# Expert layers of a macaron network: the rows of the last two items added to the residual by TensorE products

## Chip, cores and metric

The kernel runs on one core of one Trainium2 chip. The metric is the time of one execution on the device, in microseconds (us); lower is better. Five engines work on their own instruction streams and wait for each other by semaphores: TensorE (PE in the profile, its weight loads PEld), VectorE (DVE), ScalarE (ACT), GpSimd (POOL) and SyncE (SP, which here only issues DMAs).

## What is computed

The input x has 1024 tokens of 256 values, all float32. Six layers follow one another, each adding to the residual x:

```
x = x + 0.5 * L0_ffn(layernorm(x))     # expert layer 0
x = x +       L0_attn(layernorm(x))    # attention, 32 heads of 8
x = x + 0.5 * L0_ffn(layernorm(x))     # expert layer 1, same weights
x = x + 0.5 * L1_ffn(layernorm(x))     # sparse ffn
x = x +       L1_attn(layernorm(x))    # state space layer
x = x + 0.5 * L1_ffn(layernorm(x))     # sparse ffn
```

The change lies in the two expert layers:

```
logits = 30 * tanh(x @ w_gate / 30);  probs = softmax(logits)
mask = one_hot(top_k(probs, 2)).sum;  weights = probs * mask
for e in range(8):
    h = silu(x @ w1[e]) * (x @ w3[e])            # 256 -> 512
    out = out + h @ w2[e] * weights[:, e:e+1]    # 512 -> 256
```

## The kernel before, in words

The residual `xres` stays in SBUF as [128, 8, 256]: 8 tiles of 128 tokens. `moe_layer` (line 175) is called twice, as moe0 and moe1. Only the two chosen experts of each token are computed. The 2048 pairs of token and expert are sorted by expert into items of 128 rows; each expert's last item is padded, so there are at most `ITEMS` = 2048/128 + 8 - 1 = 23 items, and always 23 are computed. The column `token[:, i]` holds the number of the token of each row of item i (numbers from 1024 on are spare rows, for padding), `slot_w[:, i]` half the router's weight of each row.

Five instruction streams make up the layer. SyncE copies the residual to the DRAM tensor `sums` (L262), loads the weights, and at the end waits until all additions have landed (L269) and loads `sums` back into `xres`, two tiles in each of four DMAs (L271). GpSimd gathers the rows of an item from the normalized tokens in DRAM (L283), four items ahead, and adds the 128 result rows of an item to `sums` with one indirect, accumulating DMA (L293). An addition waits for y of its item and for the landing of the addition before it, since two items can hold the same token.

TensorE runs a loop over items that is written out by hand: gate products of item i, transposes of h of item i - 1 (`turn_h`, L576), transposes of x of item i + 1 (`turn_x`, L548), up products of item i, `down` products of item i - 1 (L584). After the loop come `turn_h` and `down` of item 22. Gate and up are three products each of split float32 parts (L62 to L64). `down` is four products of 128x128 by 128x256 in float32; each of them is two records in the trace. ScalarE applies silu (L481), copies the turned h (L487) and the high part of x (L475). VectorE makes the low part of x (`low_x`, L412), the product of silu and up (`product`, L421), and y = out * slot_w (`weigh`, L430), in the order low_x(i + 1), product(i), weigh(i - 1). There are two buffers of y; y of item i waits until addition i - 2 has landed. For the first items VectorE also splits weights (L407). At the end VectorE makes `weigh` of item 22, waits for each of the four reloads and makes the statistics of its two tiles for the next layer's norm (`token_stats`, L75). Then the block ends: all engines meet, GpSimd clears the layer's semaphores (L48), and the next layer begins with the norm (L111 to L118 in attention, L149 its first TensorE work).

A form of the same sum that the scan layer uses at its own end, an addition out of PSUM into the residual and the statistics of two tiles behind it, stands at L2286 and L75.

## Time and profile before

| | us |
|---|---|
| median of 3 timed runs | 1625.67 |
| lowest and highest of them | 1623.10, 1629.16 |
| the profiled execution | 1630.07 |
| its span in the profile | 1628.3 |

| engine | busy us | share of the span |
|---|---|---|
| TensorE, products | 1423.7 | 87% |
| TensorE, weight loads | 1052.3 | 65% |
| VectorE | 1139.8 | 70% |
| ScalarE | 878.0 | 54% |
| GpSimd | 496.3 | 30% |

The span is the time from the first to the last instruction of one profiled execution. The page of the profile gives the busy time of each engine; the timeline lists instructions in the order of their starts, consecutive ones of the same kind merged; windows give busy times within a stretch. "PEclk" is the granted clock of TensorE as a share of full speed. "x8" counts the instructions merged in a row; in square brackets stands how long the engine had been idle and what ended it. Busy shares over the span don't tell what a change in one stage is worth; that is read from the stage's own timeline.

### The profile page before, as it was taken

The page shows a single profiled execution, that of the slowest core. Times are in us where ns is not written, and L with a number is a line of the kernel's source. Part 1 is how long each engine was busy: PE and PEld are TensorE (multiplying, and loading weights), DVE is VectorE, ACT ScalarE, POOL GpSimd, SP SyncE. Part 2 cuts the span into 40 slices and gives each one's busy share as a digit, 9 for nine tenths or more (in the row PEclk, how much of TensorE's full clock was granted, in tenths as well). Part 3 has the DMA queues.
Part 4 walks back from the last instruction along what each step waited for, and adds up shares of the span by engine and source line. Part 5 has one row for each costly group of instructions (what it writes and reads, how often), then busy time and mean ns, then how long its engine had stood idle before and what let it go on. Part 6 is the DMA issues. An engine that isn't in the chain of part 4 may idle for free. (4 is left out here: it accounts for less than half of the span.)

```text
span 1628.3 us, 25033 instructions
## 1 busy us (share of the span) xinstructions
PE 1423.7 (87%) x7896; PEld 1052.3 (65%) x7896; DVE 1139.8 (70%) x2026; ACT 878.0 (54%) x1238; POOL 496.3 (30%) x407
## 2 busy tenths in 40 slices
PE   2999489999999965997697987899999999999697
PEld 2788333333333335886585876788888888888586
DVE  6532599998989946522675684887878778778475
ACT  2422227776767744421433775767666666765432
POOL 1444110000000021543100013565657566565200
PEclk7999759999999976999798898999999999999899
DMA  8533211111111009323201002322222223231200
GB/s 294 155 53 46 59 32 16 25 25 25 28 26 27 8 10 363 54 47 60 82 1 34 26 23 85 97 79 98 78 98 91 84 90 97 78 97 53 78 1 26
DMA packets 83020, 111.92 MB, mean 69 GB/s; under 512 B 11904, under 2 KB 60800, under 8 KB 82912
## 3 DMA queue, kind: packets, MB, share of 16 engines
q1 hardware_dynamic: 73152, 96.05, 19.6%
q0 software_dynamic: 9376, 14.16, 4.9%
q8 instruction: 52, 0.85, 0.2%
q10 hardware_dynamic: 384, 0.39, 0.1%
q14 instruction: 56, 0.46, 0.1%
HBM read 89.99 MB, written 11.93 MB: 63 GB/s over the span
## 5 line engine op out<-in xcount | busy, mean ns | idle before, releaser
L962 DVE TENSOR_REDUCE attn_max_chunks<-attn_scores 128x1 f32<-128x512 f32 x488 | 305.1, 683 | 31.9 <-PE attn_scores L1213 26.5
L1124 ACT ACTIVATE attn_probs<-attn_scoresT 128x1024 f32<-128x1024 f32 x256 | 248.2, 1022 | 121.0 <-PE attn_scoresT L1229 120.8
L1213 PE MATMUL attn_scores<-attn_k_picks,attn_q_group 64*128 64x512 f32 x488 | 189.4, 468 | 14.3 <-DVE attn_max_chunks L962 6.0
L1213 PEld LDWEIGHTS attn_scores<-attn_k_picks,attn_q_group 64*128 64x128 f32 x488 | 86.1, 192 | 178.3 <-DVE attn_max_chunks L962 170.4
L1644 DVE SCALAR_TENSOR_TENSOR ssm_scan_x<-ssm_scan_proj,ssm_w_conv,ssm_scan_x 128x1023 f32<-128x1023 f32 (+2 forms) x96 | 123.0, 1282 | 56.9 <-ACT ssm_scan_x L1639 51.2
L1229 PE MATMUL attn_scoresT<-attn_q_group,attn_k_picks 64*128 64x512 f32 x512 | 155.2, 441 | 3.2 <-ACT attn_probs L1124 3.2
L1241 PE MATMUL attn_o<-attn_probs,attn_v_group 128*32 128x512 f32 x1024 | 139.7, 618 | 0.4 <-ACT attn_probs L1124 0.3
L62 PE MATMUL ssm_scan_proj<-ssm_xnT_hi,ssm_w_in_hi 128*128 128x512 f32 x256 | 110.6, 432 | 18.1 <-DVE ssm_scan_x L1644 16.1
L293 POOL DMA_INDIRECT moe_sums<-moe_xn,moe_token x46 | 78.2, 1699 | 128.9 <-DVE moe_xn L430 118.6
L1639 ACT ACTIVATE ssm_scan_x<-ssm_scan_proj,ssm_b_conv,ssm_w_conv 128x1024 f32<-128x1024 f32 x32 | 38.5, 1205 | 138.6 <-DVE ssm_scan_v L2268 135.5
L481 ACT ACTIVATE moe_xnT<-moe_gate 128x512 f32<-128x512 f32 x46 | 27.5, 598 | 154.2 <-PE moe_gate L64 154.2
L64 PE MATMUL ssm_scan_proj<-ssm_xnT_hi,ssm_w_in_lo 128*128 128x512 f32 x256 | 102.7, 401 | 0.0
L63 PE MATMUL ssm_scan_proj<-ssm_xnT_lo,ssm_w_in_hi 128*128 128x512 f32 x256 | 102.1, 399 | 0.0
L2504 PE MATMUL ssm_scan_out<-ssm_scan_w_out,ssm_scan_v 128*128 128x256 f32 x448 | 101.3, 379 | 0.0
L2167 POOL TENSOR_TENSOR ssm_scan_c_exp_cum<-ssm_cT,ssm_scan_exp_cum 128x896 f32<-128x896 f32 x32 | 68.9, 2153 | 72.6 <-PE ssm_scan_y L2465 71.7
L883 POOL TENSOR_TENSOR attn_max_parts<-attn_max,attn_zeros 128x16 fp32r<-128x16 f32 x16 | 3.6, 222 | 286.2 <-DVE attn_max L957 286.2
L2504 PEld LDWEIGHTS ssm_scan_out<-ssm_scan_w_out,ssm_scan_v 128*128 128x128 f32 x448 | 83.0, 190 | 10.1
L1229 PEld LDWEIGHTS attn_scoresT<-attn_q_group,attn_k_picks 64*128 64x128 f32 x512 | 80.0, 190 | 14.1 <-ACT attn_probs L1124 8.9
L584 PE MATMUL moe_out<-moe_w_down,moe_xn 128*128 x368 | 87.1, 379 | 1.5 <-ACT moe_xn L487 1.5
L2175 POOL TENSOR_TENSOR ssm_scan_x_to_end<-ssm_scan_x_dt,ssm_decay_to_end 128x512 f32<-128x512 f32 x64 | 83.5, 1324 | 0.6 <-DVE ssm_scan_x_dt L2232 0.6
L412 DVE TENSOR_TENSOR moe_in_row<-moe_xT,moe_in_row 128x256 fp32r<-128x256 f32 x46 | 19.5, 424 | 85.9 <-ACT moe_in_row L475 85.5
L2252 DVE SCALAR_TENSOR_TENSOR ssm_scan_states<-ssm_scan_states,ssm_chunk_decay,ssm_scan_turn 128x128 f32<-128x128 f32 x192 | 66.7, 347 | 17.9 <-DVE ssm_scan_states L2252 3.3
(361 smaller groups left out, 3403.2 us busy)
## 6 DMA issues: line engine op xcount, KB each, us to landing
ssm_cum_all<-ssm_cums SPq DMA_DIRECT2D x32, 512.0 KB, 3.8
ssm_scan_exp_cum<-ssm_cums SPq DMA_DIRECT2D x32, 512.0 KB, 3.7
moe_w_gate_lo<-in_moe_w SPq DMA_DIRECT2D x16, 512.0 KB, 11.2
moe_w_up_lo<-in_moe_w SPq DMA_DIRECT2D x16, 512.0 KB, 11.1
moe_w_down<-in_moe_w SPq DMA_DIRECT2D x16, 512.0 KB, 11.3
ssm_w_in<-in_in_w SPq DMA_DIRECT2D x64, 128.0 KB, 2.5
ssm_scan_w_out<-in_out_w SPq DMA_DIRECT2D x7, 512.0 KB, 3.8
moe_sums<-main_residual SPq DMA_DIRECT2D x2, 1024.0 KB, 5.6
```

The costliest lines, as they stand in the source:

```text
L62: nc.tensor.matmul(out, lhs_hi, rhs_hi, start=start, stop=False)
L63: nc.tensor.matmul(out, lhs_hi, rhs_lo, start=False, stop=False)
L64: return nc.tensor.matmul(out, lhs_lo, rhs_hi, start=False, stop=stop)
L584: last = nc.tensor.matmul(out_ps[i % 2][:, 0:D].unsqueeze(1), hT[i % 2][:, k, :], w_dn[:, bass.ds(e * KI + k, 1), :], start=(k == 0), stop ...
L962: return nc.vector.tensor_reduce(rmaxc[:, half, place:place + 1], chunk_bank(g, n), AX_X, ALU.max).then_inc(reduced, 1)
L1124: nc.scalar.activation(probs[s % 2][:, 2 * pair:2 * pair + 2, :], st_ps[pair][:], ACT.Exp, scale=SCALE).then_inc(exp_done, 1)
L1213: nc.tensor.matmul(chunk_bank(g, n), qs[b][head_rows(j), t * P:(t + 1) * P], kz[b][head_rows(j), j % 2, c * BANK:(c + 1) * BANK], start=Tr ...
L1229: last = nc.tensor.matmul(st_ps[pair][:, i, :], kz[b][head_rows(j), j % 2, kt * P:(kt + 1) * P], qs[b][head_rows(j), half_cols(half)], sta ...
L1241: last = nc.tensor.matmul(o_ps[j * STACK:(j + 1) * STACK, :], vg[b][:, kt, :], probs[s % 2][:, i, :], start=(kt == 0), stop=(kt == KT_TILE ...
L1644: return nc.vector.scalar_tensor_tensor(out[:, shift:], ps[:, :S - shift], w(k), out[:, shift:], ALU.mult, ALU.add)
L2175: nc.gpsimd.tensor_tensor(xend[:, cs, :], xdt[:, cs, :], to_end[:, cs, bass.ds(n, 1)] .broadcast_to([P, cs.stop - cs.start, PD]), ALU.mult ...
L2504: last = nc.tensor.matmul(out[:, m, :], v[:, v_row(b * NORM_HEADS + jn), cols], w_out[:, jn, :], start=(jn == 0), stop=(jn == NORM_HEADS - 1))
```

## The change

Items 21 and 22 are no longer added by GpSimd to `sums`; `ADDED` = 21 items are, and SyncE's reload waits for 21 additions. For the last two items VectorE makes, in the rounds of items 8 and 9, a matrix `to_rows` of ones and zeros for each of the eight tiles of tokens: row p of the item and column n is one if row p belongs to token n of the tile. It takes the place of tiles that are no longer in use. TensorE multiplies these with y of the item, 8 products for each item, and sums both items in four banks of PSUM, two tiles in each: those of item 21 ahead of `down` of item 22, those of item 22 behind it. VectorE then adds the banks to the reloaded `xres`, tile by tile, before the statistics of each pair.

```diff
+ON_CHIP = 2
+ADDED = ITEMS - ON_CHIP
...
+        token_f = sp.sb("token_f", [P, ON_CHIP])
+        to_rows = [in_row[:].rearrange("p a n -> p (a n)")[:, S:2 * S], send[:].rearrange("p a c n -> p (a c n)")[:, 0:S]]
...
+        row_banks = [up_ps[1], gate_ps[1], gate_ps[0], up_ps[0]]
...
-            sync.wait_ge(summed, 16 * ITEMS)
+            sync.wait_ge(summed, 16 * ADDED)
...
             for i in range(ITEMS):
-                add_rows(i)
+                if i < ADDED:
+                    add_rows(i)
                 if i + AHEAD < ITEMS:
                     gather(i + AHEAD)
...
+            def rows_of(m):
+
+                if m == 0:
+                    dve.wait_ge(q["token_done"], 1)
+                    nc.vector.tensor_copy(token_f[:], token[:, ADDED:ITEMS]).then_inc(q["token_f_done"], 1)
+                    dve.wait_ge(q["token_f_done"], 1)
+                for t in range(TT):
+                    last = nc.vector.tensor_scalar(to_rows[m][:, t * P:(t + 1) * P], route["places"][:], token_f[:, m:m + 1],
+                                                   -float(t * P), ALU.subtract, ALU.is_equal)
+                last.then_inc(q["to_rows_done"], 1)
+
+            def add_here(t):
+                n = t // 2
+                dve.wait_ge(reloaded[n], 16)
+                dve.wait_ge(q["rows_done"], n + 1)
+                bank = row_banks[n]
+                nc.vector.tensor_tensor(xres[:, t, :], bank[:, (t % 2) * D:(t % 2 + 1) * D], xres[:, t, :], ALU.add
+                                        ).then_inc(q["rows_added"], 1)
...
+                if EXPERTS <= i < EXPERTS + ON_CHIP:
+                    rows_of(i - EXPERTS)
             weigh(ITEMS - 1)
             for n in range(TT // 2):
-                dve.wait_ge(reloaded[n], 16)
+                for t in (2 * n, 2 * n + 1):
+                    add_here(t)
+                dve.wait_ge(q["rows_added"], 2 * n + 2)
                 token_stats(nc, stats, xres, (2 * n, 2 * n + 1))
...
+            def to_tokens(i):
+                m = i - ADDED
+                pe.wait_ge(q["to_rows_done"], m + 1)
+                pe.wait_ge(q["y_done"], i + 1)
+                if m == 0:
+                    pe.wait_ge(q["silu_done"], ITEMS)
+                    pe.wait_ge(q["h_done"], ITEMS)
+                for n, bank in enumerate(row_banks):
+                    for half in range(2):
+                        t = 2 * n + half
+                        last = nc.tensor.matmul(bank[:, half * D:(half + 1) * D], f32(to_rows[m][:, t * P:(t + 1) * P]), y[i % 2][:],
+                                                start=(m == 0 and half == 0), stop=(m == ON_CHIP - 1), skip_group_check=True)
+                    if m == ON_CHIP - 1:
+                        last.then_inc(q["rows_done"], 1)
+
             turn_h(ITEMS - 1)
+            to_tokens(ADDED)
             down(ITEMS - 1, e_before)
+            to_tokens(ADDED + 1)
```

## Rows read from the trace of the kernel before

**Rows 1.** The page: busy us, share of the span and instructions of each engine.

```profile
PE 1423.7 (87%) x7896; PEld 1052.3 (65%) x7896; DVE 1139.8 (70%) x2026; ACT 878.0 (54%) x1238; POOL 496.3 (30%) x407
```

**Rows 2.** Windows (stretch, length, then PE, PEld, DVE, ACT, POOL busy; PEclk): expert loop.

```profile
42.00:172.00 130.00, 122.15 (x596) 102.10 (x596) 47.93 (x79) 41.87 (x80) 57.83 (x42) 0.97 0.38 78
```

**Rows 3.** Timeline (start, length, engine, line, operation) of the first expert layer's end.

```profile
163.10 0.48 DVE L430 TENSOR_SCALAR moe_xn<-moe_out,moe_slot_w 128x256 f32<-128x256 f32 x1 [0.99 <-PE moe_out L584]
163.86 1.54 POOL L293 DMA_INDIRECT moe_sums<-moe_xn,moe_token  x1 [3.41 <-DVE moe_xn L430]
164.26 1.59 PEld L584 LDWEIGHTS moe_out<-moe_w_down,moe_xn 128*128 128x128 f32 x8 [1.00 <-issue]
...
166.29 0.48 DVE L430 TENSOR_SCALAR moe_xn<-moe_out,moe_slot_w 128x256 f32<-128x256 f32 x1 [2.71 <-PE moe_out L584]
168.30 1.54 POOL L293 DMA_INDIRECT moe_sums<-moe_xn,moe_token  x1 [2.90 <-DMA moe_sums<-moe_xn,moe_token]
172.01 1.90 SPq L271 DMA_DIRECT2D main_residual<-moe_sums  x4
174.73 1.43 DVE L75 BATCH_NORM_STATS2 main_token_stats<-main_residual 128x6 f32<-128x256 f32 x4 [7.95 <-DMA main_residual<-moe_sums]
177.14 1.44 DVE L75 BATCH_NORM_STATS2 main_token_stats<-main_residual 128x6 f32<-128x256 f32 x4 [0.98 <-DMA main_residual<-moe_sums]
```

**Rows 4.** The reload's line (L271), both layers: time from issue to landing.

```profile
DMA to landing us min/median/max: 2.7/3.5/4.4
```

**Rows 5.** Timeline of two rounds of the first expert layer's loop.

```profile
150.76 1.72 PEld L584 LDWEIGHTS moe_out<-moe_w_down,moe_xn 128*128 128x128 f32 x8
...
152.92 0.48 DVE L430 TENSOR_SCALAR moe_xn<-moe_out,moe_slot_w 128x256 f32<-128x256 f32 x1 [0.98 <-PE moe_out L584]
...
155.72 0.42 DVE L412 TENSOR_TENSOR moe_in_row<-moe_xT,moe_in_row 128x256 fp32r<-128x256 f32 x1 [2.31 <-ACT moe_in_row L475]
...
157.71 0.19 PEld L62 LDWEIGHTS moe_gate<-moe_w_gate_hi,moe_in_row 128*128 128x128 f32 x1
...
158.88 1.56 POOL L293 DMA_INDIRECT moe_sums<-moe_xn,moe_token  x1 [3.62 <-DVE moe_xn L430]
```

**Rows 6.** Timeline of the second expert layer's end.

```profile
760.31 0.48 DVE L430 TENSOR_SCALAR moe_xn<-moe_out,moe_slot_w 128x256 f32<-128x256 f32 x1 [0.98 <-PE moe_out L584]
...
774.21 1.43 DVE L75 BATCH_NORM_STATS2 main_token_stats<-main_residual 128x6 f32<-128x256 f32 x4 [0.70 <-DMA main_residual<-moe_sums]
```

**Rows 7.** Timeline of VectorE: attention's norm, and the scan layer's end.

```profile
182.54 1.38 DVE L118 TENSOR_SCALAR attn_xn<-main_residual,attn_ln_mean_var,attn_ln_rstd 128x256 f32<-128x256 f32 x4
...
1513.21 0.88 DVE L2286 SCALAR_TENSOR_TENSOR main_residual<-ssm_scan_out,ssm_scan_rnorm,main_residual 128x256 f32<-128x256 f32 x2
1514.12 0.75 DVE L75 BATCH_NORM_STATS2 main_token_stats<-main_residual 128x6 f32<-128x256 f32 x2
1514.80 0.86 DVE L2286 SCALAR_TENSOR_TENSOR main_residual<-ssm_scan_out,ssm_scan_rnorm,main_residual 128x256 f32<-128x256 f32 x2
```

**Rows 8.** Groups of VectorE by line and form: busy us, mean ns of one, idle before.

```profile
L2286 DVE SCALAR_TENSOR_TENSOR main_residual<-ssm_scan_out,ssm_scan_rnorm,main_residual 128x256 f32<-128x256 f32 x60 | 26.1, 477 | 1.6 <-PE ssm_scan_out L2504 0.9
L412 DVE TENSOR_TENSOR moe_in_row<-moe_xT,moe_in_row 128x256 fp32r<-128x256 f32 x46 | 19.5, 424 | 85.9 <-ACT moe_in_row L475 85.5
L75 DVE BATCH_NORM_STATS2 main_token_stats<-main_residual 128x6 f32<-128x256 f32 x48 | 17.0, 415 | 17.9 <-DMA main_residual<-moe_sums 17.7
L341 DVE TENSOR_TENSOR moe_pick<-moe_at,route_places 128x128 f32<-128x128 f32 x2 | 0.6, 292 | 0.1
```

**Rows 9.** Timeline: TensorE's first work in the attention layer.

```profile
183.33 1.57 PEld L149 LDWEIGHTS attn_scores<-main_ident,attn_xn 128*128 128x128 f32 x8 [17.48 <-DVE attn_xn L118]
```

**Rows 10.** Windows, columns as in group 2: behind the expert layers, and in attention.

```profile
170.00:172.00 2.00, 0.00 (x0) 0.00 (x0) 0.00 (x0) 0.00 (x0) 0.00 (x0) 0.59 0.60 66
...
186.00:188.00 2.00, 1.97 (x9) 1.59 (x8) 2.00 (x4) 1.17 (x2) 0.00 (x0) 0.64 0.00 0
...
188.00:200.00 12.00, 10.42 (x63) 9.26 (x62) 11.32 (x32) 2.71 (x10) 0.00 (x0) 1.00 0.07 15
...
210.00:220.00 10.00, 10.00 (x18) 4.72 (x17) 10.00 (x18) 0.00 (x1) 1.08 (x1) 0.50 0.07 14
...
790.00:792.00 2.00, 2.00 (x7) 1.49 (x7) 0.73 (x1) 1.98 (x3) 2.00 (x2) 0.60 0.00 0
```

More of the change, by code:

```diff
@@ L250, in moe_layer @@
                  "x_turned", "xT_done", "xT_lo_done", "w_hi_done", "w_lo_done", "gate_done", "up_done", "silu_done", "h_done", "h_turned",
-                 "hT_done", "out_done", "y_done")
+                 "hT_done", "out_done", "y_done", "token_f_done", "to_rows_done", "rows_done", "rows_added")
         q = {n: sp.sem(n) for n in names}
```

## Prediction, made before the changed kernel was run

> **What bounds the kernel now.** I read the busy shares first. TensorE is busy for 87% of the span [rows 1]. A share over the whole span says nothing about a change that touches two places of some 16 us, so I cut the span into stages. In the expert loop of the first expert layer (42 to 172 us) TensorE is busy 122 of 130 us [rows 2]. So the loop is bound by TensorE, and its end, the part that the change is about, by something else: from 166.3 to 183.33 TensorE does nothing [rows 3, 9].
>
> The timeline shows by what [rows 3]. The last rows y of item 21 are made by VectorE at 163.10, of item 22 at 166.29. GpSimd issues addition 21 at 163.86. Addition 22 could start at 166.77, when y is ready, but it starts at 168.30: it waits for addition 21 to land. The reload is issued at 172.01, that is 3.71 us after the last addition's start. The first statistics start at 174.73, 2.72 us later, and the last end at 177.14 + 1.44 = 178.58. The second layer has the same end, from 760.31 to 775.64 [rows 6]. From y of item 21 (163.58) to the last statistics the chain is 15.0 us long, and from y of item 22 it is 11.8 us: addition 21's landing, one addition, one reload, four pairs of statistics. Almost all of it is transfers' latency, with no engine busy.
>
> **What the change removes.** The additions of items 21 and 22 go, and the reload waits for addition 20, which starts at 158.88 in the loop [rows 5]. With the 3.71 us of the last addition it has landed at 162.6, so the reload's four issues are over by 164.5. The latest landing seen for one of the eight reloads is 4.4 us after its issue [rows 4], so the fourth (issued at about 164.0) is there by 168.4. All of the reload moves under TensorE's work. Behind SP's wait nothing else is queued in this layer, and GpSimd has nothing left after addition 20. These are free as long as the first sum below is later than 168.4.
>
> **What it adds in the loop.** For two items VectorE makes eight 128x128 comparisons each, behind y of items 7 and 8, before the next low part of x. The trace has no such TENSOR_SCALAR; the nearest are a 128x128 TENSOR_TENSOR with 292 ns [rows 8] and 128x256 TENSOR_SCALARs, four of which take 1.38 us with 0.41 for the last, so (1.38 - 0.41)/3 = 0.324 us from start to start [rows 7]. Eight cost 1.6 us (at 0.2) to 2.4 us (at 0.292, taken one after another), plus 0.2 us for the copy of the token numbers. VectorE waits 2.31 us there for the next copy of x, in every round [rows 5]; the low part that follows ends at 156.14 and the next item's first weights are loaded at 157.71, so 1.5 us more is spare. Cost nothing; without this cover it would be up to 5 us per layer once. GpSimd's gathers and additions are issued from another engine and aren't behind these.
>
> **What it adds at the end.** TensorE now has, per item, eight products of 128x256 float32. The same form is `down`, whose four products are eight records in the trace; its eight weight loads take 1.72 us with 0.19 for the last, so (1.72 - 0.19)/7 = 0.219 us from record to record [rows 5]. Eight products are 16 records, 3.50 us. Steps of the first layer:
> 1. y of item 21 is ready at 163.10 + 0.48 = 163.58. TensorE, which has finished the transposes of h by then, starts 0.06 us later (VectorE's second xn is over at 182.54 + 0.324 + 0.41 = 183.27, the weight load that waits for it starts at 183.33 [rows 7, 9]): 163.64.
> 2. Its 16 records are over at 167.14. `down` of item 22 stood at 164.26 before and is now behind them in TensorE's queue: 2.88 us later. This is the price of the order; the wait for y of item 21 has this product queued behind it, and everyone waits for that.
> 3. From the start of `down`'s weight loads to VectorE's y takes 2.03 us at the old end (164.26 to 166.29 [rows 3]) and 2.16 in the loop, where the loads follow other work (150.76 to 152.92 [rows 5]); I take 2.16. y of item 22: 169.30 to 169.78 (before: 166.77).
> 4. TensorE starts the products of item 22 at 169.84. The first pair of tiles is four of the records, 2.03 - 4 x 0.219 = 1.15 us to the first addition on VectorE: 171.0. That is 2.6 us later than the reload's latest landing, so the transfers are hidden. The further pairs come every 0.88 us.
> 5. VectorE does two additions and two statistics for each pair. The scan layer's tail does the same with a slightly dearer addition: from pair to pair 1514.80 - 1513.21 = 1.59 us [rows 7]. A plain TENSOR_TENSOR of this size out of PSUM takes 0.42 us instead of 0.48 [rows 8], so 1.48 to 1.59 a pair. As 1.5 is more than 0.88, VectorE sets the pace: 4 pairs are 6.0 to 6.4 us, I take 6.2. The end is 177.2.
>
> Before it was 178.58: 1.4 us gained. The second layer by the same steps: y of item 21 at 760.79, products until 764.35, y of item 22 at 766.99, first addition 768.2, end 774.4, before 775.64 [rows 6]: 1.2 us gained. Together 2.6 us. What comes after the block (end barrier, first work of the next layer 1 to 2 us later) has the same length.
>
> On VectorE's pace, rows and a page differ. The row shows xn's operations 0.324 us apart though one lasts 0.41 [rows 7]: they overlap. The Trainium skill ("VectorE: DVE Perf Modes", section "The DRAIN you can't avoid") says that the next operation doesn't start until the pipe is empty, and its later section on two instructions with no wait between them lets them start earlier. By the first rule a pair would be the plain sum of durations and the gain of each layer about 0.5 us smaller. The trace speaks for the second.
>
> **The rivals.**
> (a) The tail gives the gain back: nothing measurable, or slightly slower. The place is the item-22 products, which now start after a pause of TensorE (its `down` ends at about 169.2, products at 169.84). If the granted clock falls before them, each record takes twice as long, 0.43 us: 16 x 0.43 = 6.9 us, the last pair is done at 177.0 and the end comes at 178.7 instead of 177.2. If VectorE's operations don't overlap on top (sum of durations 2 x 0.42 + 2 x 0.41 = 1.67 us a pair [rows 8], 0.12 more than I took), another 0.5. That is 3 to 4 us in two layers against a gain of 2.6: 1630.5 to 1631.5 by the profile, up to 1.4 us slower than before. It decides at 15.0 us: if y of item 21 to the last statistics takes longer than that, the change loses. Against: the clock fell at about 170 (0.59 over 170 to 172) when TensorE had stopped at 166.25 [rows 3, 10], over 4 us later, and the new pause is 0.6 us.
> (b) The next layer starts at the full clock. TensorE's idle stretch to the attention layer shrinks from 17.1 us (166.25 to 183.33) to about 8.4 us (173.5 to 181.9), in front of the ffn layer from 15.6 to about 7 us. Before, the clock came back between 186 and 188 (0.64 there, 1.00 behind it), and between 790 and 792 [rows 10], in each case some 4 us after TensorE had begun again. If it stayed up, the first 4 us of TensorE's work in each layer would be shorter by up to 2 us: 2.6 + 4 = 6.6, profile 1623.5. Against: before, it fell well within the idle stretch (already at 170 to 172), and most of the stretch remains. The Trainium skill's "TensorE: Matmul & The Clock Gate", section "Part 1: The HAM clock gate", has the clock go to half after idleness and come back after sustained work, at a moment that varies from run to run; by that rule (b) doesn't happen, and the moment of return scatters.
> (c) The clock comes back later in the attention layer, because all is shifted. What speaks for it: over 210 to 220 us the trace shows the half clock while TensorE is reported busy throughout [rows 10]. If the same happened at the start and it stayed at half over 188 to 200 us, where TensorE is busy 10.4 of 12 us [rows 10], up to 8 us (VectorE, busy 11.3 us there, would hide the rest) would be lost: profile 1635.5, 5.4 us slower than before. It decides at whether the clock is full by 190.
> (d) The change doesn't do what it says, since something other than the reload's wait orders the end, such as `y`'s own wait for additions: y of item 22 needs addition 20, landed by 162.6, and y of item 21 needs addition 19, a round earlier. Neither binds. I give this no time of its own.
>
> **How the numbers follow.** The profiled run took 1630.07 us with a span of 1628.3; the median of the three timed runs is 1625.67, 4.4 less. I carry that distance over: 1630.07 - 2.6 = 1627.5 in a profile, 1625.67 - 2.6 = 1623.1 as the median, a change of 0.16%. The bounds of the sum: with 1.67 us a pair both layers gain 0.9 + 0.7 = 1.6 us, with 1.48 us and 2.03 for `down` 1.7 + 1.5 = 3.2, so 1622.5 to 1624.1; the three runs of before alone spread over 1623.1 to 1629.16, and a median of a few such runs adds 2 to 3 us either way. Chances: forecast 0.72, (a) 0.14 at 1626.1 to 1627.1 as a median, (b) 0.06 at 1619, (c) 0.05 at 1631, others 0.03. The range reaches over (a) and (b) and half of the runs' spread: 1617 to 1630. About 0.5% (8.1 us) is what a measurement of this kernel can tell from no change. None of the cases reaches it by its mechanism alone; with scatter I give faster 0.05, slower 0.03, and 0.92 to neither.
>
> **What would show it.** In the changed profile: SP's reload issued at about 162.6 in the first layer (before 172.01) and as much earlier in the second; 16 records of products between y of item 21 and `down` of item 22, `down` about 2.9 us later than before relative to the transposes; y of item 22 3.0 us later; VectorE's first addition 1.15 us after the item-22 products start, waiting for TensorE and not for a DMA; then four pairs 1.5 to 1.6 us apart; the last statistics 1.2 to 1.4 us earlier, counted from y of item 21 (13.6 instead of 15.0 us). The comparisons would stand in VectorE's gap and the loop's 5.2 us a round would be unchanged. Wrong: a reload that lands after 171; the half clock in the item-22 products; a round that grows at items 8 to 10; a difference of several us that lies outside the two ends.

## The result

Before and after were timed in turn on one chip, five runs each:

| | median us | runs | ratio to before, 95% interval |
|---|---|---|---|
| before | 1625.67 | 1623.1 to 1630.91 | |
| changed | 1612.53 | 1610.7 to 1617.29 | 0.9901 (0.9876 to 0.9925) |

The change makes the kernel 13.1 us faster. I had forecast 2.6 us, with a range of 1617 to 1630; the measured time lies outside it. The profiled run took 1612.53 us, its span is 1610.7 us and the mean granted clock 0.952 (before 0.933). The page of after: the span, the busy shares, and the granted clock in 40 slices. The busy shares answer to [rows 1]; the clock line of before follows them in a fence of its own.

```profile
span 1610.7 us, 25224 instructions
...
PE 1433.5 (89%) x7960; PEld 1064.1 (66%) x7960; DVE 1152.7 (72%) x2076; ACT 877.9 (55%) x1238; POOL 489.1 (30%) x403
...
PEclk9999869999999976999899998999999999999899
```

```profile
PEclk7999759999999976999798898999999999999899
```

TensorE is busy 10 us more than before and VectorE 13 us more, and the span is 17.6 us shorter. (The medians differ by 13.1 us; a single pair of traces carries some us of scatter.) The clock lines differ by one or two tenths in six slices: the first, the two from 163 to 244 us, the one from 773 us and the two from 855 to 936 us. A slice is 40.7 us long, which is too coarse for what follows: the slices with the stalls that are found below, at about 370 and 460 us, read 9 in both.

### The profile page after: what moved, and what is told of

It is laid out like the page before. It is cut to its first block and busy times, and to the rows that moved or that the text cites. A ratio compares the mean times of both kernels' runs of the same rounds, so it can differ in the third digit from the quotient of the medians.

```text
span 1610.7 us, 25224 instructions
## 1 busy us (share of the span) xinstructions
PE 1433.5 (89%) x7960; PEld 1064.1 (66%) x7960; DVE 1152.7 (72%) x2076; ACT 877.9 (55%) x1238; POOL 489.1 (30%) x403
## 5 line engine op out<-in xcount | busy, mean ns | idle before, releaser
L299 POOL DMA_INDIRECT moe_sums<-moe_xn,moe_token x42 | 71.6, 1706 | 114.9 <-DVE moe_xn L437 110.2
L2551 PEld LDWEIGHTS ssm_scan_out<-ssm_scan_w_out,ssm_scan_v 128*128 128x128 f32 x448 | 83.8, 192 | 10.4
L2413 ACT ACTIVATE ssm_scan_decay<-ssm_cum_all,ssm_neg_cum 128x128 f32<-128x128 f32 x256 | 77.8, 386 | 0.0
```

The costliest lines, as they stand in the source:

```text
L2551: last = nc.tensor.matmul(out[:, m, :], v[:, v_row(b * NORM_HEADS + jn), cols], w_out[:, jn, :], start=(jn == 0), stop=(jn == NORM_HEADS - 1))
```

## The two ends: what the prediction was about

The first expert layer's end in the changed kernel, answering to [rows 3], in four pieces of the timeline: y of item 21, the reload's issue, TensorE's weight loads, and VectorE from y of item 22 on (start, length, engine, line, operation, count, idle before and its releaser):

```profile
165.26 0.48 DVE L437 TENSOR_SCALAR moe_xn<-moe_out,moe_slot_w 128x256 f32<-128x256 f32 x1 [0.98 <-PE moe_out L614]
```

```profile
164.75 1.90 SPq L277 DMA_DIRECT2D main_residual<-moe_sums  x4
```

```profile
165.81 0.73 PEld L649 LDWEIGHTS moe_up<-moe_xn,moe_in_row 128*128 128x128 f32 x4 [0.39 <-issue]
...
169.16 1.70 PEld L614 LDWEIGHTS moe_out<-moe_w_down,moe_xn 128*128 128x128 f32 x8
...
171.90 0.73 PEld L649 LDWEIGHTS moe_up<-moe_xn,moe_send 128*128 128x128 f32 x4 [1.04 <-issue]
```

```profile
171.30 0.48 DVE L437 TENSOR_SCALAR moe_xn<-moe_out,moe_slot_w 128x256 f32<-128x256 f32 x1 [5.56 <-PE moe_out L614]
173.14 0.76 DVE L455 TENSOR_TENSOR main_residual<-moe_up,main_residual 128x256 f32<-128x256 f32 x2 [1.36 <-PE moe_up L649]
173.93 0.75 DVE L75 BATCH_NORM_STATS2 main_token_stats<-main_residual 128x6 f32<-128x256 f32 x2
174.60 0.74 DVE L455 TENSOR_TENSOR main_residual<-moe_gate,main_residual 128x256 f32<-128x256 f32 x2
...
178.26 0.75 DVE L75 BATCH_NORM_STATS2 main_token_stats<-main_residual 128x6 f32<-128x256 f32 x2
```

All of this block sits 2.16 us later in the span than before, so times are counted from the start of y of item 21. The reload is issued 0.51 us before that (before the change 8.9 us after it) and nobody waits for it: VectorE's first addition waits for TensorE. The last statistics end at 178.26 + 0.75 = 179.01, that is 13.75 us after y of item 21 began. Before it was 178.58 - 163.10 = 15.48 us [rows 3]. The second layer measured 13.75 us too, before 15.33 [rows 6]. Over all the traces with the old ends this time lies between 14.9 and 15.7 us. The two ends are 3.3 us shorter. That is near the forecast 2.6, and a quarter of the 13.1 us.

The comparisons stand in VectorE's gap, as foreseen. VectorE's timeline of after:

```profile
98.29 1.74 DVE L446 TENSOR_SCALAR moe_send<-route_places,moe_token_f 128x128 fp32r<-128x128 f32 x8
...
100.68 0.42 DVE L419 TENSOR_TENSOR moe_in_row<-moe_xT,moe_in_row 128x256 fp32r<-128x256 f32 x1 [0.66 <-ACT moe_in_row L505]
```

Eight take 1.74 us, and VectorE's wait for ScalarE in that round shrinks from 2.31 [rows 5] to 0.66 us. The round keeps its 5.2 us.

## Where the other 10 us are

I cut both traces into the program's stages, and counted in each the packets of the queues that the profile calls "instruction", by their sizes:

```
stage                       before             changed
attention layer, us         427.5              419.2
  its 8192-byte reads       20                 10
scan layer, us              644.8              638.4
  its 16384-byte reads      22                 22
both expert layers' ends    30.8               27.5
```

The attention layer lost 8.3 us, the scan layer 6.4. In the attention layer VectorE runs a loop of three passes, and at the jump back the timeline of before has an idle time with nothing that it waits for ("issue"); the changed kernel has none. First VectorE before, then after:

```profile
364.96 0.69 DVE L962 TENSOR_REDUCE attn_max_chunks<-attn_scores 128x1 f32<-128x512 f32 x1 [0.22 <-PE attn_scores L1213]
368.33 4.28 DVE L962 TENSOR_REDUCE attn_max_chunks<-attn_scores 128x1 f32<-128x512 f32 x7 [2.67 <-issue]
...
459.29 4.28 DVE L962 TENSOR_REDUCE attn_max_chunks<-attn_scores 128x1 f32<-128x512 f32 x7 [2.64 <-issue]
```

```profile
364.86 2.48 DVE L1009 TENSOR_REDUCE attn_max_chunks<-attn_scores 128x1 f32<-128x512 f32 x4 [0.22 <-PE attn_scores L1260]
```

The DMA view of the same stretch has the second half of it. Before (365 to 377 us) three packets of an instruction queue lie behind the jump, after (364 to 376 us) there is none:

```profile
q1 hardware_dynamic: 375, 0.77, 42.2%
q14 instruction: 3, 0.02, 0.6%
```

```profile
q1 hardware_dynamic: 386, 0.80, 44.0%
```

The second jump, at 456 us, shows the same stall of 2.64 us before and none after. The two stalls are 5.3 us.

A whole pass says it more sharply. It is 278 recorded instructions on VectorE. Before, its second pass (DMA view of 365 to 457 us) reads five pieces of VectorE's code again:

```profile
q14 instruction: 5, 0.04, 0.1%
```

In the changed kernel the view of 363 to 495 us, which holds both jumps, has no instruction queue at all:

```profile
q1 hardware_dynamic: 2208, 3.35, 15.8%
```

So with the one placing of the code the loop is read anew in each pass, and with the other it is kept. The rest of the attention layer's difference goes with the clock behind them. Windows with the columns of [rows 2], before, then after:

```profile
366.00:368.00 2.00, 1.19 (x9) 0.16 (x8) 0.00 (x0) 1.79 (x3) 0.40 (x1) 1.00 0.35 53
368.00:370.00 2.00, 0.93 (x4) 0.48 (x4) 1.67 (x3) 0.16 (x1) 0.00 (x0) 1.00 0.36 53
370.00:372.00 2.00, 1.89 (x13) 0.63 (x12) 2.00 (x5) 1.83 (x2) 0.00 (x0) 0.94 0.35 47
372.00:374.00 2.00, 2.00 (x10) 1.06 (x7) 1.02 (x3) 0.06 (x1) 0.00 (x0) 0.50 0.62 100
374.00:376.00 2.00, 2.00 (x12) 0.57 (x10) 2.00 (x4) 1.94 (x2) 0.00 (x0) 0.71 0.62 103
```

```profile
370.00:372.00 2.00, 1.92 (x16) 0.74 (x14) 1.78 (x4) 1.50 (x2) 0.00 (x0) 1.00 0.34 49
372.00:374.00 2.00, 1.92 (x16) 0.85 (x8) 1.78 (x4) 1.24 (x2) 0.00 (x0) 1.00 0.62 98
374.00:376.00 2.00, 2.00 (x16) 0.83 (x15) 1.79 (x4) 1.24 (x3) 0.00 (x0) 1.00 0.63 103
```

VectorE stood still for 2.7 us from 365.6, TensorE was busy for 1.19 and 0.93 us of the next two stretches of 2 us, and some 6 us after the standstill began its granted clock is at 0.50, its lower level of 1.2 GHz. After, it stays at 1.00. All the traces of this document agree: behind each of the twelve stalls in six traces the clock is at 0.50 within 3 to 6 us of the stall's start, and in the eight traces without stalls it is full from 245 to 560 us.

From this came the theory that the experiments below test: **the change moves the code of all that follows, and a loop's jump back stalls or doesn't stall by where the loop's code lies.** The diff adds 33 instructions to VectorE's code in each expert layer, and 67 to TensorE's. A read of VectorE's queue is 8192 bytes, one of TensorE's 16384. The Trainium skill ("Runtime: NRT & Kernel Launch", section "Instruction fetch mechanics") describes the mechanism: the instruction memory is small and filled in blocks, ahead of the engine and in sequence, and a taken branch whose target isn't in the two blocks held has to wait for a read. By its figures (256 instructions in 16 KiB) 8192 bytes are 128 instructions, which gives the size of a shift that should bring the old state back. The loop's pass of 278 instructions is then more than two of VectorE's pieces, and yet it is kept in the changed kernel: counted in these pieces, more than two are held. The rival was that the shorter ends themselves, or the reload and additions that moved, give the later layers another phase and so the 10 us.

## The experiments

All the kernels, with before run in turn on the same chip as each group of three. "Reads" are those of the attention layer (8192 bytes) and the scan layer (16384 bytes). "Ends" is the time from y of item 21 to the last statistics, layers 1 and 2.

| kernel | median us | ratio to before, 95% interval | attention us, reads | scan us, reads | ends us |
|---|---|---|---|---|---|
| before again | 1625.79 (one run) | | 425.3, 20 | 645.4, 31 | 14.9 to 15.7 |
| before, +33 on VectorE | 1621.40 | 0.9967 (0.9950 to 0.9984) | 417.2, 10 | 645.2, 22 | 14.9 to 15.7 |
| changed, +95 on VectorE | 1620.82 | 0.9959 (0.9943 to 0.9974) | 423.4, 20 | 637.9, 22 | 13.75, 14.11 |
| changed, `down` of item 22 first | 1608.44 | 0.9886 (0.9861 to 0.9911) | 417.3, 10 | 636.6, 22 | 13.45, 13.45 |
| changed again | 1612.14 | 0.9900 (0.9880 to 0.9920) | 416.5, 10 | 637.4, 22 | 13.75, 13.75 |
| changed, woven order | 1609.00 | 0.9885 (0.9864 to 0.9906) | 419.2, 10 | 640.2, 22 | 11.16, 11.16 |
| changed, one item on chip | 1616.03 | 0.9924 (0.9903 to 0.9944) | 415.0, 10 | 648.5, 31 | 13.24, 13.22 |
| before, +33 VectorE, +34 TensorE | 1620.29 | 0.9955 (0.9939 to 0.9971) | 417.2, 10 | 648.0, 31 | 14.9 to 15.7 |
| before, +68 TensorE | 1623.02 | 0.9967 (0.9953 to 0.9981) | 424.5, 20 | 639.3, 22 | 14.9 to 15.7 |
| before, +33 VectorE, +68 TensorE | 1615.09 | 0.9914 (0.9891 to 0.9936) | 416.1, 10 | 641.0, 22 | 14.9 to 15.7 |
| before, third trace | 1632.24 (one run) | | 424.5, 20 | 648.2, 31 | 14.9 to 15.7 |
| changed, +95 VectorE, +61 TensorE | 1629.87 | 1.0009 (0.9990 to 1.0028) | 425.4, 20 | 644.0, 22 | 13.75, 14.10 |

The numbers with a plus are instructions in each expert layer, as the traces record them. The medians of before in the four groups were 1627.45, 1629.69, 1629.61 and 1629.06 us.

**Before again.** No edit; how stable is what I read?

> The kernel before once more, for a second trace. Theory A (code loading): the two stalls of VectorE of 2.67 and 2.64 us in the attention layer, right behind the back jumps of its loop, stand at the same places with the same length, with 8192-byte instruction reads behind each jump, and TensorE's half clock follows each. Theory B (the clock's own timing): stalls and dips of the clock lie elsewhere or are missing in this trace, and the time could be that of the changed kernel, 1612 us.

The jump of VectorE stalls again, by 2.69 and 2.71 us (first fence, VectorE's timeline). In this trace TensorE has a stall of its own, which the first trace of before didn't have: at the jump of the scan layer's loop (1246.99 us, second fence, TensorE's timeline).

```profile
367.82 4.28 DVE L962 TENSOR_REDUCE attn_max_chunks<-attn_scores 128x1 f32<-128x512 f32 x7 [2.69 <-issue]
```

```profile
1246.99 0.77 PE L62 MATMUL ssm_scan_proj<-ssm_xnT_hi,ssm_w_in_hi 128*128 128x512 f32 x1 [3.79 <-issue]
```

The DMA view of 1240 to 1256 us has TensorE's reads around it:

```profile
q8 instruction: 4, 0.07, 1.8%
```

The scan layer has 31 of these reads here and 22 in the first trace, with the same code. So at TensorE's jump the outcome differs from run to run; at VectorE's a kernel that was traced more than once had the stalls in all of its traces or in none.

**Before, with VectorE's code moved alone.** 33 memsets of one column, in the gaps of rounds 10 to 20:

```diff
+FILL = {10: 3, 11: 3, 12: 3, 13: 3, 14: 3, 15: 3, 16: 3, 17: 3, 18: 3, 19: 3, 20: 3}
+        scrap = sp.sb("scrap", [P, sum(FILL.values())])
...
+                first = sum(FILL.get(k, 0) for k in range(i))
+                for k in range(first, first + FILL.get(i, 0)):
+                    nc.vector.memset(scrap[:, k:k + 1], 0.0)
```

> The kernel before with 33 more VectorE instructions (tiny memsets of 60 ns) in each expert layer's loop, three a round, in VectorE's idle time; nothing of the change. It moves VectorE's later code by as many instructions as the change does. Theory A (code loading: before, the attention loop's jump target was out of what VectorE keeps of its code): both stalls are gone, attention is 5.3 us shorter for the stalls and 1 to 3 us more for the half clock that followed them, so 6 to 8 us faster than before, ratio 0.995 to 0.996. Theory B (clock timing, or the tail's work itself): no difference to before, ratio 1.000, the stalls stay.

Work that does nothing makes the kernel 5.4 us faster by the ratio, somewhat less than I had expected. VectorE's timeline shows no stall at the jump:

```profile
364.65 2.49 DVE L967 TENSOR_REDUCE attn_max_chunks<-attn_scores 128x1 f32<-128x512 f32 x4 [0.18 <-PE attn_scores L1218]
367.36 2.48 DVE L967 TENSOR_REDUCE attn_max_chunks<-attn_scores 128x1 f32<-128x512 f32 x4 [0.22 <-PE attn_scores L1218]
```

The expert layers are as before and only the attention layer is shorter. The rival that the shorter ends cause it is out for the attention layer.

**The changed kernel, with VectorE's code moved on by a whole block.** The same edit with 95 memsets, so that all that follows lies 33 + 95 = 128 instructions behind its old place:

```diff
+FILL = {10: 9, 11: 9, 12: 9, 13: 9, 14: 9, 15: 9, 16: 9, 17: 8, 18: 8, 19: 8, 20: 8}
```

> The changed kernel with 95 more VectorE instructions in each expert layer's loop, so that with the 33 of the change VectorE's later code is moved by 128 in each layer. Reads of instructions on that queue are 8192 bytes, 128 instructions of 64 bytes, so its blocks lie as before. Theory A: the stalls of 2.6 to 2.7 us stand behind both jumps again; about 7 us of the 13 are lost, ratio to before 0.993 to 0.997, and what remains is the two tails, 3.3 us. Theory B: it stays at the changed kernel's time, ratio 0.990.

VectorE's timeline at the first jump:

```profile
366.51 3.68 DVE L1014 TENSOR_REDUCE attn_max_chunks<-attn_scores 128x1 f32<-128x512 f32 x6 [2.78 <-issue]
```

The stalls are back (2.78 and 2.69 us), with 20 reads, and more than half of the change's gain is lost. So it is not the added instructions that remove the stalls but where they put the loop, and this speaks for blocks of 128; shifts other than 25 (the kernel with one item), 33 and 128 weren't tried. The Trainium skill's rule, in the same section, that a jump to a target that isn't held stalls agrees with this trace; its block of 16 KiB doesn't: VectorE's reads are 8192 bytes, and a shift of 128 instructions, not 256, restores the state.

**The changed kernel, `down` of item 22 ahead of item 21's products.** This takes away the wait that I called the price of the order.

```diff
             turn_h(ITEMS - 1)
-            to_tokens(ADDED)
             down(ITEMS - 1, e_before)
+            to_tokens(ADDED)
             to_tokens(ADDED + 1)
```

> The changed kernel with the down product of item 22 ahead of the products of item 21's rows on TensorE. The price of the order in the prediction was 2.9 us before y of item 22. Now y of item 22 comes at the old place, about 3.2 us behind y of item 21 instead of 6.0; item 21's products (3.5 us) follow down and hold item 22's back until about 5.8 us after y of item 21's start, so the first addition comes some 0.5 us earlier than in the changed kernel, 7.3 us after the start of y of item 21 instead of 7.9, and 1 us in all is gained over two layers: ratio to before 0.989 to 0.990.

VectorE's timeline of the first layer's end, the two y and the first addition:

```profile
163.24 0.48 DVE L437 TENSOR_SCALAR moe_xn<-moe_out,moe_slot_w 128x256 f32<-128x256 f32 x1 [0.98 <-PE moe_out L614]
166.44 0.48 DVE L437 TENSOR_SCALAR moe_xn<-moe_out,moe_slot_w 128x256 f32<-128x256 f32 x1 [2.71 <-PE moe_out L614]
170.82 0.76 DVE L455 TENSOR_TENSOR main_residual<-moe_up,main_residual 128x256 f32<-128x256 f32 x2 [3.90 <-PE moe_up L649]
```

y of item 22 comes 3.20 us after that of item 21, 2.84 us sooner than in the changed kernel, yet the first addition comes only 0.30 us sooner (7.58 against 7.88), since the 16 records of item 21 now stand before those of item 22. The end is 0.3 us shorter. The order costs little: the records have to be done either way. Its ratio is 0.0015 below the changed kernel's and the intervals overlap, so it isn't shown to be better.

**The changed kernel again**, beside the next three.

> The changed kernel once more, timed and traced beside the others. If the change's 13 us are the two tails (3.3 us), VectorE's code position (5 to 8 us) and something in the state space layer that all changed kernels share (3 to 6 us), the ratio is 0.989 to 0.992, no stall stands in attention, and the state space layer takes 636 to 640 us. If the last is scatter, that layer can come out at 641 to 645.

1612.14 us, 0.990: the result repeats in a second group of runs, and both ends are 13.75 us again.

**Woven order.** Each bank is finished as soon as it can be:

```diff
+            def to_tokens(i, banks):
...
+                for n in banks:
+                    bank = row_banks[n]
...
+            to_tokens(ADDED, (0,))
             down(ITEMS - 1, e_before)
+            to_tokens(ADDED, (1,))
+            to_tokens(ADDED + 1, (0, 1))
+            for n in (2, 3):
+                to_tokens(ADDED, (n,))
+                to_tokens(ADDED + 1, (n,))
```

> The changed kernel with TensorE's end in another order: item 21's products for the first two tiles, down of item 22, item 21's for the second two, item 22's for the first four, then items 21 and 22 for each pair in turn. TensorE's work from y of item 21 to the end is 1.8 us of down and 7.0 us of products with no pause; the first addition no longer waits for all products of item 21. By the prediction's step prices the first addition starts 5.9 us after the start of y of item 21 (7.9 in the changed kernel, 7.6 with down first), the last statistics end at 12.0 us instead of 13.7, so 3 to 4 us in two layers: ratio 0.987 to 0.989 to before. If VectorE's additions and statistics alone set the end (4 x 1.45), the gain is no more than the 2 us by which the first addition comes earlier, each layer.

The same three operations in VectorE's timeline:

```profile
162.63 0.48 DVE L437 TENSOR_SCALAR moe_xn<-moe_out,moe_slot_w 128x256 f32<-128x256 f32 x1 [0.99 <-PE moe_out L614]
166.09 0.48 DVE L437 TENSOR_SCALAR moe_xn<-moe_out,moe_slot_w 128x256 f32<-128x256 f32 x1 [2.97 <-PE moe_out L614]
167.93 0.76 DVE L455 TENSOR_TENSOR main_residual<-moe_up,main_residual 128x256 f32<-128x256 f32 x2 [1.36 <-PE moe_up L650]
```

The first addition comes 5.30 us after y of item 21, and the end is 11.16 us, 2.6 shorter than in the changed kernel in each layer. Of these 5.2 us the medians show 3.1 (1612.14 to 1609.00). It is the version I would keep, by its trace; by times alone it isn't told apart from the changed kernel. Its order adds 8 further waits to TensorE's code in each layer, so that code doesn't lie where the changed kernel has it.

**One item on chip** instead of two, with `down` before its products:

```diff
-ON_CHIP = 2
+ON_CHIP = 1
...
-            to_tokens(ADDED)
             down(ITEMS - 1, e_before)
-            to_tokens(ADDED + 1)
+            to_tokens(ADDED)
```

> Only item 22 goes by TensorE's products; GpSimd adds item 21, and the reload waits for 22 additions. By the rows of before, addition 21 lands 5 us after the start of y of item 21 and the reload's first part 2.7 us later, so VectorE's first addition starts at 7.7 to 7.9 us, now ended by the reload and not by TensorE (whose first products are ready at 4.9 us). The tail is as long as with two items, 13.0 to 14.0 us, if that holds, and the second item on TensorE buys nothing: ratio 0.989 to 0.992. If the reload's four parts, 4.4 us each at the latest, come later than VectorE wants them, the tail grows by up to 1 us a layer: 0.991 to 0.993.

VectorE's timeline, the first addition:

```profile
170.38 0.75 DVE L455 TENSOR_TENSOR main_residual<-moe_up,main_residual 128x256 f32<-128x256 f32 x2 [3.70 <-DMA main_residual<-moe_sums]
```

Now the first addition waits for the reload (the releaser is a DMA). It starts 7.38 us after y of item 21, 0.5 us sooner than in the changed kernel, and the ends are shorter by as much. But the median is 3.9 us above that of the changed kernel, though its attention layer is without stalls too. Its scan layer has 31 reads, stalls of 2.54 and 1.45 us at TensorE's jump, and 648.5 us. Its TensorE code is moved by 34 instructions a layer, half as much as in the changed kernel (one item's products instead of two).

**Before, with VectorE's code moved and TensorE's by half.** Written as 67 waits for a count long reached, behind the last `down`:

```diff
             down(ITEMS - 1, e_before)
+            for _ in range(67):
+                pe.wait_ge(q["expert_done"], 1)
```

> The kernel before with the 33 VectorE memsets of each expert layer and, behind TensorE's last down product of each layer, 67 waits on a semaphore that is long set: as many TensorE instructions as the change adds, in its idle time and without work. What is open is why the state space layer takes 637 to 638 us in the three changed kernels' traces and 645 in the three of before's kind. Theory C (TensorE's code position): it falls to 638 here, time 7 us below the 33-filler kernel, ratio to before 0.991 to 0.993. Theory D (scatter of the clock's dips, or something in the tail that reaches further): 645 as before, ratio 0.995 to 0.998, same as the 33-filler kernel.

Two successive waits go into one instruction, so this moved TensorE's code by 34 in each layer, and the test I had meant wasn't made. What it shows by chance is half the shift: 31 reads, stalls at the scan loop's jump, and a scan layer of 648.0 us, as in the kernel with one item.

**Before, with TensorE's code alone moved as in the change**: the same edit with 134 waits and without the memsets. The trace has 68 more instructions of TensorE in each layer; the change adds 67.

> TensorE's shift alone: the kernel before with the 134 waits in each expert layer. Theory C: attention as before, 425 to 427 us with VectorE's two stalls and 20 reads of 8192 bytes; the state space layer with 22 reads of 16384 bytes and 637 to 642 us; ratio 0.997 to 0.999. Theory D: 22 or 31 reads as it falls, 0.998 to 1.001.

At the jump TensorE's timeline has no gap:

```profile
1242.82 1.04 PE L2440 MATMUL ssm_scan_turn<-main_ident,ssm_scan_x 128*128 128x128 f32 x8
1243.62 0.47 PE L62 MATMUL ssm_scan_proj<-ssm_xnT_hi,ssm_w_in_hi 128*128 128x512 f32 x1
```

The scan layer is 639.3 us, the attention layer keeps both stalls (2.76, 2.66) and its 424.5 us. The waits themselves (0.108 us apart, 7.2 us in all) lie in TensorE's idle stretch of 17 us behind the last `down`.

**Before, with both engines' code moved as in the change**: 33 memsets and 134 waits, the ends as they were.

> As the kernel before with 33 VectorE memsets and TensorE waits in each expert layer, but 134 waits; in the last trace of this kind 67 waits had made only 34 TensorE instructions, half of what the change adds, so this is now the change's shift (67 a layer) on both engines, with the old tails. Theory C (TensorE's code position): the state space layer's loop is never loaded anew (22 reads of 16384 bytes in the layer, not 31), its time loses the 4 to 5 us that a reload costs in about half of before's executions, and with VectorE's 5 to 8 us the ratio is 0.991 to 0.995; by adding the two tails of 3.3 us one comes to the changed kernel. Theory D (scatter of the clock's dips only): 31 reads can appear, ratio 0.995 to 0.998.

0.9914 without any of the change's work: 14.0 us of 1629.61. This is the run that decides. The change's ratio is 0.990.

**Before, a third trace.**

> The kernel before a third time, one look. The first trace had 22 reads of 16384 bytes in the state space layer and no stall behind its jump, the second 31 reads and a stall of 3.8 us with the same code. If that is a race between TensorE's reading ahead and the jump, either can come here. VectorE's two stalls in attention stand in every trace of this code.

31 reads, a gap of 3.88 us at TensorE's jump, the stalls of VectorE at 2.71 and 2.66 us: two traces of before in three have the jump's stall on TensorE, all three have VectorE's.

**The changed kernel, with both engines' code back at the old place in the blocks**: 95 memsets as above, and 61 instructions on TensorE ahead of the first gathered rows.

```diff
             pe.wait_ge(q["expert_done"], 1)
+            for _ in range(122):
+                pe.wait_ge(q["both_done"], 1)
             turn_x(0)
```

> The changed kernel with the code of both engines behind the expert layers back where it was: 95 memsets on VectorE in each expert layer (128 instructions a layer with the change's 33), and on TensorE 122 waits in each, two to an instruction, so 61 instructions of 0.108 us, put where TensorE waits 7.6 us for the first gathered rows. With the 134 that the change adds in two layers TensorE's code is moved by 256 in all. If code position is what the change gained beside its tails, this shows the change's own work alone: both stalls of VectorE in attention, 22 or 31 reads in the state space layer, tails of 13.75 us instead of 15.4, so 3.3 us faster than before, ratio 0.998, interval within 0.996 to 1.000. If the change gains in some other way too, it stays at 0.996 or below.

1.0009 (0.999 to 1.0028), where I had expected 0.998: with the whole of the change's work in it, the kernel is as fast as before. Its ends are (15.48 - 13.75) + (15.33 - 14.10) = 3.0 us shorter, and the times don't show this gain. The inserted waits don't seem to be free here. In layer 1 y of item 21 comes at 169.07 us, 3.8 us later than in the changed kernel (165.26) and later than in each of the thirteen other traces (162.3 to 165.9); in layer 2 it is 1.2 us later, which is within their scatter. If some 4 us are the waits' price, the kernel would without them be some 2 to 3 us faster than before, which is what the ends give. That is an estimate from one trace and isn't shown. VectorE's timeline has the stall again:

```profile
373.12 2.48 DVE L1016 TENSOR_REDUCE attn_max_chunks<-attn_scores 128x1 f32<-128x512 f32 x4 [2.78 <-issue]
```

**The sum.** VectorE's position is worth 0.33% (5.4 us), TensorE's 0.33% (5.4 us) and both together 0.86% (14.0 us, interval 10.4 to 17.8 us), the ends 3.3 us by the trace; the change itself 1.0% (16.3 us against before's median of its group, 13.1 in the first comparison). By stages: six traces whose attention layer has 20 reads take 425.1 us there on average, eight with 10 reads 417.2, a difference of 7.9, of which the stalls are 5.3 to 5.5. The scan layer takes 645.5 us on average with TensorE's code at the old place (five traces), 648 with half the shift (two), 638.7 with the shift of the change or its like (seven).

**What stays open.** Where the scan layer has 31 reads, the stall at its loop's jump (3.8 to 5.2 us) explains about half of the difference to 638.7 us. But before's first trace, the one with 33 memsets and the last kernel have 22 reads and no stall at the jump, and their scan layers still take 644 to 645 us. They lose it in pieces within the first 170 us of the layer, with stretches at the half clock: there the mean granted clock is 0.88 to 0.89 in the five traces at the old place and 0.89 to 0.91 in the seven with the shift. I didn't find what begins them, nor did I try the other positions in a block. So it is shown that TensorE's code position is worth the 6.8 us (the run with 68 TensorE instructions alone has 639.3 us there, and a shift of 256 in all brings 644.0 back), and not by which steps. Nor did I find why one and the same code reads ahead of the jump in some runs and late in others.

## Why the prediction was wrong

- **What bounds the ends** held. The chain of transfers is gone, and nothing waits for the reload: its landings took 2.6 to 4.1 us (row below, answering to [rows 4]), the four issues are over at 164.75 + 1.90 = 166.65, so the last is there by 170.8, and the first addition starts at 173.14.

```profile
DMA to landing us min/median/max: 2.6/3.6/4.1
```

- **The loop** held: comparisons and copy are hidden (idle 2.31 to 0.66 us), GpSimd and SP have nothing behind.
- **Step 1 and 2** held: the products start 0.07 us behind y of item 21 (forecast 0.06), and 16 records precede `down` (165.81 to 169.16, 3.35 us, forecast 3.50).
- **Step 3**: y of item 22 comes 6.04 us after that of item 21 (forecast 6.20).
- **Step 4**: the first addition at 7.88 us, as forecast (7.9). In part that is luck: the products of item 22 start 0.06 us later behind their y than I took and need 0.09 us more to the first addition (173.14 - 171.90 = 1.24 us), which makes up for step 3.
- **Step 5**: pairs are 1.45 us apart (173.14, 174.60, 176.04, 177.49), and I took 1.55 from a range of 1.48 to 1.59. Two additions together last 0.74 to 0.76 us though one lasts 0.42: they overlap, more than I allowed. This is the mis-sized term: 0.3 us a layer. On VectorE's pace the trace spoke right, against the first of the two rules that the prediction quotes from the Trainium skill ("VectorE: DVE Perf Modes", section "The DRAIN you can't avoid").
- **The sum of the ends**: 13.27 us from y's end, forecast 13.6; gains of 1.7 and 1.6 us, forecast 1.4 and 1.2.
- **Rival (a)**, half clock in the products of item 22: no. The clock is full through the whole end and falls behind it. **Rival (b)**, full clock in the next layer: no. It is at 0.50 over 180 to 182 us and returns at 190, after TensorE's work has begun; before, it returned between 186 and 188. So (b) is out. **(c)**, a later return, was to decide at whether the clock is full by 190, and it is full from there; but it comes back some 6 us after TensorE's first work (183.80) and before it was some 4 us, so a little of (c) is in this trace. Windows of after, columns as above:

```profile
178.00:180.00 2.00, 0.00 (x0) 0.00 (x0) 0.97 (x3) 0.00 (x0) 0.13 (x1) 0.90 0.00 0
...
188.00:190.00 2.00, 2.00 (x8) 2.00 (x7) 1.16 (x2) 0.30 (x2) 0.00 (x0) 0.54 0.00 0
190.00:192.00 2.00, 1.74 (x11) 1.43 (x10) 1.81 (x6) 0.23 (x2) 0.00 (x0) 1.00 0.00 0
```

- **The step that failed** is one sentence: "What comes after the block (end barrier, first work of the next layer 1 to 2 us later) has the same length." The sum had no term for instructions as code. I counted what each added instruction costs where it runs, and not that it moves what stands behind it. That length changed with the code's place: moving both engines' code in the old kernel, without any of the change's work, gives 14.0 us (10.4 to 17.8), and the ends give 3.3. About 10 of the 13 us came in by that gap, and no rival had it. The trace of before showed it: a gap of 2.67 us with the releaser "issue" at a loop's first instruction, twice, and packets of an instruction queue right behind. With those rows a rival "the stalls of the attention loop go" at 5 to 8 us was to be had; which way a shift of 33 moves it, the rows of before alone don't tell. The last item of what I called wrong, a difference that lies outside the two ends, was the one to come true.

## What to carry to other kernels

An edit that adds or removes instructions ahead of a loop moves the loop in the blocks in which code is read, and on this kernel that alone was worth 0.9%, some four times the 3.3 us that the edit did by its work. So before a change is credited with a per cent, put the same number of idle instructions into the old kernel in its place, count in the trace that they are the same number, and compare. In a profile, look at the first instruction behind each loop's jump for an idle time that ends with "issue", and at instruction packets next to it: a gap there is a cost to be had by moving code, and a risk in every forecast.

## What the runs showed of the hardware that I had not expected

- A jump back whose target had to be read stalled VectorE by 2.64 to 2.78 us (twelve times in six traces; in all three traces of before and in neither of the two of the changed kernel), and TensorE by 3.8 to 5.2 us at the scan loop (in four traces; two of them are of before, whose first trace has no such stall).
- The same loop of 278 instructions was read anew in each pass at one place of its code (20 reads in the attention layer) and kept at another (10 reads, none between 363 and 495 us).
- Behind each such stall of 2.7 us on VectorE the granted clock of TensorE was at 0.50, 3 to 6 us after VectorE had stopped. The stall's price is then 4 us rather than 2.7 (7.9 us for two).
- VectorE's code is read in pieces of 8192 bytes and TensorE's in pieces of 16384; a shift by 128 instructions brought VectorE's stalls back.
- Two successive waits of TensorE went into one instruction, 0.108 us from one to the next.
